# Head stacks through memory, the output projection in halves, the context laid out by features

## The chip, the cores and the metric

The kernel runs on one core of a Trainium2 chip (trn2). The metric is the device time of one execution in microseconds (us), as the median of several runs. The core has five engines with a queue each: PE (TensorE, matrix products), DVE (VectorE), ACT (ScalarE), POOL (GpSimd) and SP (SyncE, which here only starts DMA transfers). Instructions of one engine run in the order of its program and wait on semaphores for the others.

## What is computed

A cross attention with 16 heads followed by a mixture of experts, in float32, for 8 batches of 512 tokens with 512 features. Cut to what matters here (`ctx` is the context, the mask is all ones in the data):

```
q = layernorm(x) @ Wq + bq;  k = ctx @ Wk + bk;  v = ctx @ Wv + bv      # 16 heads of 32
attn = softmax(q k^T * 32**-0.5);  x = x + concat_heads(attn v) @ Wo + bo
route_prob = softmax(layernorm(x) @ Ws + bs)                            # 8 experts, each takes its best 512 of 4096 tokens
x = x + scatter_add(route_val * (gelu(xin @ W1 + b1) @ W2 + b2))
```

## The kernel before

Float32 products are made of three products of rounded parts: every operand is kept as a hi part (float32r) and a lo part (what is left), and hi*hi, hi*lo and lo*hi are summed in PSUM. ACT writes the hi part, DVE the lo part.

**Groups.** The attention part goes through 32 groups, a group being one batch and 4 of its 16 heads (128 features). For group g, `proj` makes the transposed projections qT and kT (128 features x 512 tokens, 12 matmuls each). They are then moved into *stacks* `qst` and `kst` (three of each, taken in turn): for each of the 4 heads the stack holds in partitions 0 to 95 three rows of 32: for q hi, lo, hi, and for k hi, hi, lo, so that one matmul over 97 or 99 partitions gives all three products at once, with the mask and the row maxima in the further rows. A feature of head h sits in partition 32h+d of qT and must come to partition d of the stack, so the move is a DMA.

**Per group.** 16 `max` matmuls give scores by query, DVE takes the extreme of each row (`nmax`), ACT sums the exps (`sum`, L979); the maxima go through a transpose (`rows`) and a small DMA into the q stack. Then come 16 `score` matmuls, transposed, whose exps ACT writes to `p_ring` (L991), four to each of the steps kt = 0 to 3, and `att` adds p times v into `ps_att`, four heads at a time. `divide` and `osplit` leave the group's features in `oT`. One period of the kernel is a batch of four groups.

**Output.** When all four groups of batch b are done, `out` (48 matmuls in four tiles of 128 tokens) multiplies oT by Wo, DVE adds the residual, SP stores the sum, DVE normalises in place (`x1_norm`, which waits until the store has landed), and the routing logits follow (`route`, `logits`, `back`).

**Order.** All engines read one list of steps, the agenda, and each performs its own part of every step. A function places the steps of projections, output, loads and transposes at times given as fractions of a group (`K_AT`, `Q_AT`, `LATE_AT` and so on), between the fixed pattern of `score` and `att`. PSUM has one bank for `att` and seven that all other steps take in turn. In the period of the rows below, the late steps of batch 3 stand in group 16, the loads and transposes for batch 5 in groups 17 and 18, and the q stack of group 20, the first of batch 5, is made in group 18.

**Queues.** SP starts the q stack (L713 and L717), the stores `out_x` (L751) and `hn_rows` (L757), and the passage of the softmax denominators through memory (`rden`). POOL starts the k stack (L887, L891) and the loads of x and of the context, adds the bias to the residual (L843) and does the inverse roots of the norms (L782).

## Time and profile before

| | |
|---|---|
| median of 3 runs | 1889.41 us (1887.9 to 1889.69) |
| profiled execution | 1890.99 us, its span 1889.2 us |
| PE, DVE, ACT, POOL busy | 87%, 58%, 52%, 24% of the span |
| attention part | about 0 to 1090 us, a period of 129.7 us per batch |
| expert part | the rest |

The span is that from the first to the last instruction in the trace. "busy" does not say that an engine binds: what matters is in which stage it stands, and what ends its wait. A matmul's duration holds its latency; how fast they follow one another is seen in their starts.

### The profile page before, as it was taken

To read this page: it belongs to the slowest core of one execution; us is meant where nothing else is said; L and a number is where in the kernel's file an instruction comes from. 1 tells how busy PE (TensorE), PEld (TensorE's weight loads), DVE (VectorE), ACT (ScalarE), POOL (GpSimd) and SP (SyncE) were. 2 spreads that over 40 slices of the span, in tenths; PEclk is the share of its full clock that TensorE was granted. 3 is DMA by queue.
4 is the path that set the end of the run, shared out by engine and by line. 5 is a ranking of instruction groups with operands and counts; after the bars stand their busy time and mean duration, and the time that the engine had idled before them with its cause. 6 is when DMAs were issued, how large, how long until landed. Compare 5 with 4: busy or idle time off the path is not lost.

```text
span 1889.2 us, 22557 instructions
## 1 busy us (share of the span) xinstructions
PE 1648.3 (87%) x7795; PEld 1172.2 (62%) x7795; DVE 1097.1 (58%) x1918; ACT 985.9 (52%) x2111; POOL 455.7 (24%) x729
## 2 busy tenths in 40 slices
PE   5778978979879889798798737999999999999996
PEld 4545645536545556455364326878888888888885
DVE  5565675665665756756656364777645554455543
ACT  3688587687686785876876611222323232222321
POOL 4232332423324323324233102010202020202001
PEclk9788998989989989999899957999999999999998
DMA  4233332433424333324334213243434242515331
GB/s 158 80 98 82 101 112 63 132 90 80 146 53 122 106 82 106 107 63 129 92 81 130 85 51 112 90 118 112 140 110 141 90 139 90 163 67 162 95 106 23
DMA packets 122538, 193.99 MB, mean 103 GB/s; under 512 B 25020, under 2 KB 59472, under 8 KB 122424
## 3 DMA queue, kind: packets, MB, share of 16 engines
q1 hardware_dynamic: 93560, 125.79, 20.6%
q0 software_dynamic: 28864, 66.75, 14.0%
q8 instruction: 63, 1.03, 0.2%
q14 instruction: 51, 0.42, 0.1%
HBM read 116.03 MB, written 25.58 MB: 75 GB/s over the span
## 4 chain that ended last, share of the span: by engine, by line
PE 68%; DVE 9%; ACT 9%; issue 4%; DMA 4%; SPq 3%; POOL 1%; ACTq 0%; DVEq 0%; POOLq 0%
PE ps_gen L652 8%; PE ps_gen L654 8%; PE ps_gen L653 8%; PE ps_gen L1695 6%; PE ps_gen L1697 6%; PE ps_gen L1696 6%; PE ps_gen L1513 5%; ACT ps_gen L979 5%; PE ps_att L1544 5%; PE ps_gen L1533 4%; ACT p_ring L991 3%; PE ps_gen L1499 2%; PE ps_gen L1500 2%; DVE nmax L1151 2%; PE ps_gen L1501 2%
## 5 line engine op out<-in xcount | busy, mean ns | idle before, releaser
L1151 DVE TENSOR_REDUCE nmax<-ps_gen 128x1 f32<-128x512 f32 x512 | 338.7, 682 | 140.7 <-PE ps_gen L1513 139.0
L979 ACT ACTIVATE ps_gen<-ps_gen,nmax 128x512 f32<-128x512 f32 x512 | 342.3, 671 | 134.8 <-DVE nmax L1151 133.1
L991 ACT ACTIVATE p_ring<-ps_gen,keep_scale 128x512 f32<-128x512 f32 x512 | 339.1, 693 | 87.4 <-PE ps_gen L1533 85.7
L1041 ACT ACTIVATE gel<-ps_gen,b_cols 128x512 f32<-128x512 f32 x128 | 88.3, 690 | 450.7 <-PE ps_gen L654 450.6
L1513 PE MATMUL ps_gen<-kst,qst 97*128 97x512 f32 x512 | 231.0, 466 | 75.6 <-issue 51.6
L1398 DVE TENSOR_TENSOR gel_lo<-gel,gel_hi 128x512 fp32r<-128x512 f32 x126 | 87.2, 692 | 288.3 <-ACT gel_hi L1042 288.3
L1513 PEld LDWEIGHTS ps_gen<-kst,qst 97*128 97x128 f32 x512 | 104.4, 205 | 175.9 <-issue 121.1
L1533 PE MATMUL ps_gen<-qst,kst 99*128 99x512 f32 x512 | 192.1, 426 | 18.1 <-DMA qst<-by_row 11.9
L652 PE MATMUL ps_gen<-hT_hi,w_hi 128*128 128x512 f32 x512 | 203.1, 397 | 1.5 <-DVE hT_lo L1391 1.5
L654 PE MATMUL ps_gen<-hT_hi,w_lo 128*128 128x512 f32 x512 | 200.3, 391 | 0.0
L653 PE MATMUL ps_gen<-hT_lo,w_hi 128*128 128x512 f32 x512 | 200.3, 391 | 0.0
L1695 PE MATMUL ps_gen<-w_hi,gel_hi 128*128 128x512 f32 x504 | 198.3, 393 | 0.0
L887 POOL DMA_DIRECT2D kst<-kT_hi x256 | 126.8, 503 | 296.0 <-ACT kT_hi L962 160.6
L1697 PE MATMUL ps_gen<-w_hi,gel_lo 128*128 128x512 f32 x504 | 196.6, 390 | 0.0
L1696 PE MATMUL ps_gen<-w_lo,gel_hi 128*128 128x512 f32 x504 | 196.4, 390 | 0.0
L927 POOL DMA_INDIRECT out_x<-y_out,idx x32 | 55.7, 1740 | 583.3 <-ACT y_out L1061 504.8
L1544 PE MATMUL ps_att<-p_ring,v_sb 128*32 128x512 f32 x1024 | 147.4, 649 | 5.0 <-ACT p_ring L991 4.8
L1533 PEld LDWEIGHTS ps_gen<-qst,kst 99*128 99x128 f32 x512 | 97.0, 198 | 49.0 <-issue 21.6
L979 ACT ACTIVATION_READ_ACCUMULATOR ps_gen<-ps_gen,nmax 128x1 f32 x512 | 109.8, 214 | 0.0
L652 PEld LDWEIGHTS ps_gen<-hT_hi,w_hi 128*128 128x128 f32 x512 | 96.7, 189 | 21.0 <-issue 1.9
L654 PEld LDWEIGHTS ps_gen<-hT_hi,w_lo 128*128 128x128 f32 x512 | 96.6, 189 | 20.8
L653 PEld LDWEIGHTS ps_gen<-hT_lo,w_hi 128*128 128x128 f32 x512 | 96.7, 189 | 19.4
(199 smaller groups left out, 2777.5 us busy)
## 6 DMA issues: line engine op xcount, KB each, us to landing
w_raw<-in_L_ffn_W SPq DMA_DIRECT2D x128, 512.0 KB, 4.3
kst<-kT_hi POOLq DMA_DIRECT2D x256, 64.0 KB, 1.9
qst<-qT_hi SPq DMA_DIRECT2D x256, 64.0 KB, 2.4
x_in<-in_x POOLq DMA_DIRECT2D x60, 256.0 KB, 3.3
kst<-kT_lo POOLq DMA_DIRECT2D x128, 64.0 KB, 2.2
qst<-qT_lo SPq DMA_DIRECT2D x128, 64.0 KB, 2.0
rden_b<-rden_rows SPq DMA_DIRECT2D x32, 256.0 KB
out_x<-x_in SPq DMA_DIRECT2D x32, 256.0 KB, 2.1
```

The costliest lines, as they stand in the source:

```text
L652: e.matmul(psum, lhsT=wh, rhs=mh, start=(i == 0), stop=False)
L653: e.matmul(psum, lhsT=wh, rhs=ml, start=False, stop=False)
L654: last = e.matmul(psum, lhsT=wl, rhs=mh, start=False, stop=(i == n - 1))
L979: e.activation(psum[:, :], psum[:, :], ACT.Exp, bias=nmax[g % 2][:, c], scale=-1.0, accum_out=den[g % 2][:, c]).then_inc(drained_sem("max" ...
L991: e.activation(p_ring[n % NP_][:, :], ps("score", g, kt, h)[:, :], ACT.Exp, scale=keep_scale[:, b:b + 1]).then_inc(drained_sem("score", g, ...
L1151: e.tensor_reduce(nmax[g % 2][:, h * TB + t:h * TB + t + 1], ps("max", g, h, t)[:, :], AX.X, ALU.min).then_inc(s_min, 1)
L1513: e.matmul(ps("max", g, h, t)[:, :], lhsT=qst[k][0:ROWS_MAX, h, t * P:(t + 1) * P], rhs=kst[k][0:ROWS_MAX, h, :], start=True, stop=True).t ...
L1533: e.matmul(ps("score", g, kt, h)[:, :], lhsT=kst[k][0:ROWS_ALL, h, kt * P:(kt + 1) * P], rhs=qst[k][0:ROWS_ALL, h, :], start=True, stop=Tr ...
L1544: last = e.matmul(ps_att[h * DH:(h + 1) * DH, :], lhsT=v_sb[:, kt, (c4 * HG + h) * DH:(c4 * HG + h + 1) * DH], rhs=p_ring[((g * KT + kt) * ...
L1695: e.matmul(ps_y[tt], lhsT=gh, rhs=wh, start=(j == 0), stop=False)
L1696: e.matmul(ps_y[tt], lhsT=gh, rhs=wl, start=False, stop=False)
L1697: return e.matmul(ps_y[tt], lhsT=gl, rhs=wh, start=False, stop=(j == NF - 1))
```

## The change

It has three parts and new numbers in the placing. **Stacks:** each projection is stored in two DMAs of 128 x 512 (hi, lo) to a buffer `qk_rows` in device memory, two of them in turn for q and for k, and comes back in three loads of 32 x 4 x 512 that lay the heads beside each other; it was eight hi and four lo copies of 32 x 512 from SBUF to SBUF. The loads wait until the store has landed. **Halves:** `outa` makes the product of the first two feature blocks of a batch in its groups r = 2 and after, and DVE adds it to the residual; `out` makes the second two, and has 6 matmuls per tile instead of 12. **Context:** it is handed over transposed by the host, so each 128 x 512 tile of features is split by ACT and DVE straight from its landing place (`csplit`), without the transposes on PE.

```diff
+            if step[0] == "proj_lo":
+                self.add("stack", *step[1:])
...
-    K_AT = ((0.07, 0.17), (0.04, 0.22), (0.03, 0.15), (-0.07, 0.33))
-    Q_AT = ((0.33, 0.45), (0.23, 0.27), (0.33, 0.45), (0.12, 0.43))
+    K_AT = ((0.07, 0.38), (-0.04, 0.22), (0.05, 0.15), (-0.07, 0.18))
+    Q_AT = ((0.41, 0.43), (0.23, 0.27), (0.33, 0.37), (0.14, 0.35))
...
-    RECIP_AT, RDEN_AT, RDEN_IN_AT = 0.0, 0.05, 0.6
+    RECIP_AT, RDEN_AT, RDEN_IN_AT = -0.02, 0.28, 0.75
...
-    LATE_AT = (("residual", 0.05), ("add_bias", 0.2), ("out", 0.32), ("x1_norm", 0.44),
-               ("route", 0.57), ("logits", 0.68), ("back", 0.74))
+    HALF_AT, HALF_FOR = (("residual", 0.25), ("add_bias", 0.34), ("outa", 0.49)), 0.79
+    LATE_AT = (("out", 0.13), ("x1_norm", 0.46), ("route", 0.57), ("logits", 0.66), ("back", 0.74))
...
+        if r == 2:
+            for kind, at in HALF_AT:
+                place(i, (at, at + HALF_FOR), [(late, kind, b, t) for t in range(TB)])
...
-    for t in range(TB):
-        a.residual(B - 1, t)
-    for t in range(TB):
-        a.add("add_bias", B - 1, t)
...
+        def keep_rows(e, on, w, g):
+
+            if g >= 2:
+                on.wait_ge(s_stack_hi[w][(g - 2) % NST], 32 * ((g - 2) // NST + 1))
+                on.wait_ge(s_stack_lo[w][(g - 2) % NST], 16 * ((g - 2) // NST + 1))
+            kept = qk_rows["qk".index(w), g % 2]
+            on.wait_ge(s_proj_hi[w], g + 1)
+            e.dma_start(kept[0], raw(qk[w, "hi"][:, :])).then_inc(s_kept_hi[w], 16)
+            on.wait_ge(*drained("proj", w, g))
+            e.dma_start(kept[1], raw(qk[w, "lo"][:, :])).then_inc(s_kept_lo[w], 16)
+
+        def load_stack(e, on, w, g):
+
+            k = g % NST
+            stack, rows_hi, row_lo = (qst, (0, 2), 1) if w == "q" else (kst, (0, 1), 2)
+            kept = [qk_rows["qk".index(w), g % 2, n].rearrange("(h d) s -> d h s", d=DH) for n in range(2)]
+            on.wait_ge(s_ones_rows[k], 2)
+            if g >= NST:
+                on.wait_ge(*full("score", g - NST, KT - 1, HG - 1))
+            on.wait_ge(s_kept_hi[w], 16 * (g + 1))
+            for r in rows_hi:
+                e.dma_start(raw(stack[k][r * DH:(r + 1) * DH, :, :]), kept[0]).then_inc(s_stack_hi[w][k], 16)
+            on.wait_ge(s_kept_lo[w], 16 * (g + 1))
+            e.dma_start(raw(stack[k][row_lo * DH:(row_lo + 1) * DH, :, :]), kept[1]).then_inc(s_stack_lo[w][k], 16)
...
+                elif kind == "csplit":
+                    b, c = at
+                    on.wait_ge(*tile_landed("c", b, c))
+                    if b > 0:
+                        on.wait_ge(*full("proj", "k", b * GB - 1))
+                        on.wait_ge(*full("v", b - 1, TB - 1))
+                    e.activation(cT[0][:, c, :], tile_in("c", b, c), ACT.Copy).then_inc(s_c_hi, 1)
...
-                        on.wait_ge(*full("out", b - 1, TB - 1))
+                        on.wait_ge(*full("outa" if c4 < GB // 2 else "out", b - 1, TB - 1))
...
+                elif kind == "outa":
+                    b, t = at
+                    n, x1 = b * TB + t, x_in[residual_slot(b, t)]
+                    on.wait_ge(*full("outa", b, t))
+                    on.wait_ge(s_x1, n + 1)
+                    e.tensor_tensor(x1[:, :], ps("outa", b, t)[:, :], x1[:, :], ALU.add).then_inc(drained_sem("outa", b, t), 1)
```

How this moves PE between the last q projection of group 20 and the first max of that group. Before (L1501 is the last matmul of the projection, L1513 max, L1533 score, L1544 att, L1520 the transpose of the maxima; the last row is the first max of group 20):

```order
L1501 MATMUL ps_gen<-xT_hi,wq_lo 128x512
L1513 MATMUL ps_gen<-kst,qst 128x512
L1533 MATMUL ps_gen<-qst,kst 128x512 x2
L1513 MATMUL ps_gen<-kst,qst 128x512
L1544 MATMUL ps_att<-p_ring,v_sb 32x512 x4
L1513 MATMUL ps_gen<-kst,qst 128x512
L1533 MATMUL ps_gen<-qst,kst 128x512 x2
L1520 MATMUL ps_gen<-ident,nmax 16x128
L1533 MATMUL ps_gen<-qst,kst 128x512 x2
L1513 MATMUL ps_gen<-kst,qst 128x512
```

Of the change, from the att step of the same stretch on (max is now L1545, score L1565, att L1576, and L1592 to L1594 are outa; ahead of the rows shown stand three max and three score matmuls behind the projection, and one max; each outa tile has the three lines twice):

```order
L1545 MATMUL ps_gen<-kst,qst 128x512
L1576 MATMUL ps_att<-p_ring,v_sb 32x512 x4
L1592 MATMUL ps_gen<-wo_hi,oT_hi 128x512
L1593 MATMUL ps_gen<-wo_lo,oT_hi 128x512
L1594 MATMUL ps_gen<-wo_hi,oT_lo 128x512
...
L1545 MATMUL ps_gen<-kst,qst 128x512
L1565 MATMUL ps_gen<-qst,kst 128x512 x2
L1552 MATMUL ps_gen<-ident,nmax 16x128
L1565 MATMUL ps_gen<-qst,kst 128x512 x2
L1592 MATMUL ps_gen<-wo_hi,oT_hi 128x512
...
L1545 MATMUL ps_gen<-kst,qst 128x512
```

Two tiles of outa now stand between the projection and the max, and one more max and score matmul. On SP's queue around the q stack of group 18, before:

```order
L751 DMA out_x<-x_in0 128x512
L713 DMA qst0<-qT_hi 32x512 x8
L717 DMA qst0<-qT_lo 32x512 x4
L757 DMA hn_rows<-x_in0 128x512
L751 DMA out_x<-x_in1 128x512
L738 DMA rden_b<-rden_rows 128x1x512
L757 DMA hn_rows<-x_in1 128x512
```

Of the change:

```order
L771 DMA out_x<-x_in0 128x512
L749 DMA rden_rows<-by_row 16x128
L739 DMA kst0<-mask_rows 1x4x512
L771 DMA out_x<-x_in1 128x512
L612 DMA qk_rows<-qT_hi 128x512
L614 DMA qk_rows<-qT_lo 128x512
L626 DMA qst0<-qk_rows 32x4x512 x2
L628 DMA qst0<-qk_rows 32x4x512
L777 DMA hn_rows<-x_in0 128x512
L771 DMA out_x<-x_in2 128x512
L777 DMA hn_rows<-x_in1 128x512
L758 DMA rden_b<-rden_rows 128x1x512
```

The stack now stands behind the second store of x1 where it stood behind the first, and in front of both normalised tiles. On POOL's queue the context loads stand around the k stack of group 19 in the change like this:

```order
L848 DMA x_in2<-in_ctx_1024 128x512
L612 DMA qk_rows<-kT_hi 128x512
L614 DMA qk_rows<-kT_lo 128x512
L626 DMA kst1<-qk_rows 32x4x512 x2
L628 DMA kst1<-qk_rows 32x4x512
L848 DMA x_in3<-in_ctx_1024 128x512
L848 DMA x_in0<-in_x 128x512
```

Before, two of the four context loads stood ahead of that stack and two behind it; now three stand ahead and one behind.

## Rows read from the trace of the kernel before

**Rows 1.** The page: span, busy times, and the granted clock in 40 slices.

```profile
span 1889.2 us, 22557 instructions
PE 1648.3 (87%) x7795; PEld 1172.2 (62%) x7795; DVE 1097.1 (58%) x1918; ACT 985.9 (52%) x2111; POOL 455.7 (24%) x729
...
PEclk9788998989989989999899957999999999999998
```

**Rows 2.** Windows, stages A to D: length, busy, PEclk, DMA share, GB/s.

```profile
570.30:605.00 34.70, 32.64 (x156) 22.71 (x156) 19.83 (x36) 23.67 (x54) 12.73 (x23) 1.00 0.36 98
605.00:641.80 36.80, 32.15 (x170) 19.79 (x171) 24.15 (x52) 23.90 (x58) 13.65 (x24) 0.91 0.47 149
641.80:670.20 28.40, 23.07 (x115) 12.91 (x113) 23.38 (x46) 25.44 (x58) 10.95 (x21) 1.00 0.31 75
670.20:700.00 29.80, 23.64 (x103) 14.35 (x104) 14.67 (x24) 23.04 (x55) 6.86 (x14) 0.83 0.26 69
```

**Rows 3.** Timeline of PE in C and D: start, us, idle before in brackets.

```profile
666.03 0.39 PE L1501 MATMUL ps_gen<-xT_hi,wq_lo 128*128 128x512 f32 x1
...
667.43 1.07 PE L1544 MATMUL ps_att<-p_ring,v_sb 128*32 128x512 f32 x8
...
676.69 0.77 PE L1513 MATMUL ps_gen<-kst,qst 97*128 97x512 f32 x1 [5.72 <-issue]
...
687.04 0.40 PE L1499 MATMUL ps_gen<-cT_hi,wk_hi 128*128 128x512 f32 x1
687.27 0.40 PE L1500 MATMUL ps_gen<-cT_lo,wk_hi 128*128 128x512 f32 x1
```

**Rows 4.** Timeline of SP at the q stack of group 20.

```profile
667.54 4.99 SPq L713 DMA_DIRECT2D qst<-qT_hi  x8
672.58 2.49 SPq L717 DMA_DIRECT2D qst<-qT_lo  x4
```

**Rows 5.** Windows behind the two waits, and the one with the wait in B.

```profile
677.00:682.00 5.00, 5.00 (x16) 2.37 (x16) 2.28 (x4) 2.26 (x6) 0.00 (x0) 0.50 0.12 48
...
603.40:615.00 11.60, 7.59 (x43) 4.33 (x42) 6.03 (x14) 4.00 (x11) 4.83 (x7) 0.95 0.52 173
615.00:620.80 5.80, 5.80 (x17) 4.09 (x21) 3.18 (x6) 3.11 (x8) 0.30 (x1) 0.50 0.12 45
```

**Rows 6.** Timeline of SP at the q stack of group 18.

```profile
603.28 2.49 SPq L717 DMA_DIRECT2D qst<-qT_lo  x4
...
607.62 0.43 SPq L751 DMA_DIRECT2D out_x<-x_in  x1
```

**Rows 7.** Timeline of DVE there, and its waits from 259.4 to 1037 us.

```profile
610.71 0.55 DVE L1081 TENSOR_SCALAR x_in<-x_in,mv,rstd 128x512 f32<-128x512 f32 x1 [5.30 <-DMA out_x<-x_in]
...
DVE x_in L1081 <- DMA out_x<-x_in: 32.7, 7, 5.3
```

**Rows 8.** Timeline of PE around that wait.

```profile
604.96 0.27 PE L1520 MATMUL ps_gen<-ident,nmax 128*16 128x128 f32 x1 [1.47 <-DVE nmax L1151]
...
614.89 0.79 PE L1513 MATMUL ps_gen<-kst,qst 97*128 97x512 f32 x1 [1.66 <-ACT ps_gen L979]
```

**Rows 9.** The page's DMA issues: count, KB each, median us from issue to landing.

```profile
x_in<-in_x POOLq DMA_DIRECT2D x60, 256.0 KB, 3.3
...
out_x<-x_in SPq DMA_DIRECT2D x32, 256.0 KB, 2.1
```

**Rows 10.** Groups by line and shape from 259.4 to 1037 us.

```profile
L1465 PE MATMUL ps_gen<-ident,x_in 128*128 128x128 f32 x176 | 27.8, 280 | 16.4 <-ACT ps_gen L979 7.5 <-DVE x_in L1081 5.0 <-DVE cT_lo L1098 3.9
...
L1218 DVE TENSOR_TENSOR x_in<-ps_gen,x_in 128x512 f32<-128x512 f32 x24 | 16.6, 690 | 36.6 <-PE ps_gen L1572 32.7 <-POOL x_in L843 3.7
```

**Rows 11.** Timeline of PE at the end of the attention part.

```profile
1073.84 0.51 PE L1556 MATMUL ps_gen<-wo_hi,oT_hi 128*128 128x512 f32 x1
...
1082.18 0.39 PE L1570 MATMUL ps_gen<-wo_hi,oT_hi 128*128 128x512 f32 x1
```

More of the change, by code:

```diff
@@ L127, in load, with csplit @@
             self.add("load", kind, b, t)
+    def csplit(self, b, c):
+        self.add("csplit", b, c)
+        self.later.append(("csplit_lo", b, c))
     def stats(self, b, t):
@@ L194, in attention_agenda @@
     a = Agenda()
-    for kind in "xc":
-        for t in range(TB):
-            a.load(kind, 0, t)
+    for t in range(TB):
+        a.load("x", 0, t)
+        a.load("c", 0, t)
     for t in range(TB):
         a.stats(0, t)
-        a.turn("c", 0, t)
+        a.csplit(0, t)
         a.flush()
-        a.turn("x", 0, t)
+        a.turn(0, t)
     a.flush()
@@ L262, in late @@
             a.out(b, t)
-        elif kind in ("route", "logits", "back"):
+        elif kind in ("outa", "route", "logits", "back"):
             a.with_bank(kind, b, t)
@@ L333, in attention_agenda @@
         a.flush()
-    for t in range(TB):
-        a.residual(B - 1, t)
-    for t in range(TB):
-        a.add("add_bias", B - 1, t)
     attend(NG - 1, KT - 1)
@@ L722, in sync_program @@
                         e.dma_start(raw(kst[k][ROW_MASK:ROW_MASK + 1, :, :]), src).then_inc(s_mask_row[k], 16)
+                elif kind == "stack" and at[0] == "q":
+                    load_stack(e, on, "q", at[1])
                 elif kind == "rden":
@@ L786, in slot_free @@
                 if was == "first":
-                    on.wait_ge(*full("turn", "x", 0, at[2]))
+                    on.wait_ge(*full("turn", 0, at[2]))
+                elif was == "load" and at[0] == "c":
+                    on.wait_ge(s_c_hi, at[1] * DC + at[2] + 1)
+                    on.wait_ge(s_c_lo, at[1] * DC + at[2] + 1)
                 elif was == "load":
-                    on.wait_ge(*full("turn", *at))
+                    on.wait_ge(*full("turn", *at[1:]))
                 elif was == "wo":
@@ L1546, in tensor_program @@
                     last.then_inc(s_av, 1)
-                elif kind == "osum":
+                elif kind in ("outa", "osum", "out"):
                     b, t = at
+                    first = {"outa": 0, "osum": GB // 2, "out": GB // 2 if b < B - 1 else GB - 1}[kind]
+                    stop = {"outa": GB // 2, "osum": GB - 1, "out": GB}[kind]
+                    key = ("outa" if kind == "outa" else "out", b, t)
                     cols = slice(t * P, (t + 1) * P)
-                    on.wait_ge(*free("out", b, t))
-                    on.wait_ge(s_ol, GB * (b + 1) - 1)
+                    if kind != "out" or b < B - 1:
+                        on.wait_ge(*free(*key))
+                    on.wait_ge(s_ol, GB * b + stop)
@@ L1575, in tensor_program @@
+                        e.matmul(ps(*key)[:, :], lhsT=oh, rhs=w_hi["o"][:, c, :], start=(c in (0, GB // 2)), stop=False)
+                        e.matmul(ps(*key)[:, :], lhsT=oh, rhs=w_lo["o"][:, c, :], start=False, stop=False)
+                        last = e.matmul(ps(*key)[:, :], lhsT=ol, rhs=w_hi["o"][:, c, :], start=False, stop=(c in (GB // 2 - 1, GB - 1)))
+                    if kind != "osum":
+                        last.then_inc(full_sem(*key), 1)
                 elif kind == "route":
@@ L1762 @@
             a = np.ascontiguousarray(a.reshape(-1, 128).T)
+        if name == 'ctx_1024':
+            a = np.ascontiguousarray(a.transpose(0, 2, 1))
         arrays[f"in_{name}"] = a
```

156 lines of the change are left out of this document (60 added, 96 removed).

## The prediction

> **What bounds the kernel now.** The page first: one execution of 1889.2 us, PE busy for 87%, and a granted TensorE clock that sags all through the first 1070 us, the attention part [rows 1]. The expert part behind it is not touched. The attention part repeats every 129.7 us, one batch of four groups of heads. I cut one period at the transposes of the row maxima and read it in windows [rows 2]: stage A (34.7 us: projections, v, two output tiles), B (36.8: two output tiles, routing, context), C (28.4: x, projections), D (29.8: projections, v of the next batch). No stage is ruled by one engine throughout. A is PE: 32.6 of 34.7. C is ACT: 25.4 of 28.4, 90%. B and D are not full on anything: B has PE 32.2, ACT 23.9 and DVE 24.2 of 36.8, D has PE 23.6 and ACT 23.0 of 29.8. So B and D hold time that a wait takes, and I looked for the waits.
>
> In D: PE ends the last q projection of the next batch at 666.4, does 3 to 4 us of other work and stands for 5.7 us before the first max matmul of that group, until 676.69 [rows 3]. The max needs all twelve stack transfers. SP issues eight for 4.99 us from 667.54 and four for 2.49 us from 672.58 [rows 4]; the first wait is 1.1 us behind PE, the stack then takes 9.15. The stall costs twice: from 677 to 682 PE is full at a granted clock of 0.50 (1.2 GHz of 2.4) [rows 5], while later, at 1.00, matmuls start 0.23 us apart [rows 3]. Five microseconds at half speed are 2.5 lost. Together 8.2 us, seven times (once per batch with a successor).
>
> In B: the same SP queue is still issuing stack transfers when an x1 tile is ready, so its store starts at 607.62 behind L717 and a store [rows 6]. DVE may normalise only when that store has landed: it stands 5.30 us, until 610.71, in front of everything queued on it, nmax reductions included [rows 7]. PE stands 1.47 us before and 1.66 behind that wait [rows 8], and 4.0 us in all from 603.4 to 615, then works 5.8 us at clock 0.50 [rows 5], 2.9 lost. DVE's wait adds up to 32.7 us in the six periods that I grouped [rows 7].
>
> **The change, part by part.**
>
> *Stacks.* q goes by SP, k by POOL: two stores of 256 KB to memory and three loads of 256 KB in place of twelve copies of 64 KB. Issue time on SP falls from 7.5 us [rows 4] to about five times 0.62, 3.1 us. The path is now two landings in series. From the nearest rows, a 256 KB store lands in 2.1 us and a load in 3.3 [rows 9]: hi store 2.1, two hi issues 1.25, then the lo load 3.3, makes 6.65 us in place of 9.15 (the lo store, begun 0.9 later, lands at 3.0 and hides). The other bound: the store of rows 6 and 7 took 3.1 us, which gives 7.65; if both landings grow by 2 us, 10.65. I take 6.65, by the medians. The k stacks have nobody waiting at present and I cost them at nothing; the cover is most of a stage. The memory traffic added, 64 times 512 KB in 1040 us, is 32 GB/s on 69 to 149 [rows 2]: nothing, except in the full part of B. The first sum stands by these rows alone.
>
> The Trainium skill speaks against this edit: "DMA: Bandwidth & Descriptors", Anatomy of one DMA, puts about 2 us fixed on each DMA and says that waiting for the write receipt can be surprisingly long when the target is HBM, which the old on-chip copies did not have. By its fit (2.0 us and bytes over 436 GB/s) a landing is 2.6 us and the path, as an estimate, 2.6 + 1.25 + 2.6 = 6.45. The rows agree in size (2.1 and 3.3); what the old path lost was issue time.
>
> *Cover of the wait in D.* Between the last q projection and the first max PE had nine 128x512 matmuls and one att step, 9 x 0.23 + 1.0 + 0.1 = 3.2 us. Now two outa tiles stand there too, and the q projections are two matmuls earlier: 24 x 0.23 + 1.1 = 6.6 us. Stack at 1.1 + 6.65 = 7.75: PE idles 1.1 instead of 5.7. I take the clock to hold there: stage A keeps 1.00 with 2.1 us of idle in it [rows 2]. D: -4.6 - 2.5, and plus 18 matmuls of outa (4.2) that now lie in D: -2.9. PE work alone of 27.8 (98 matmuls, four att steps, 1.0 small) at A's share of 0.94 would be 29.6, a floor above that; so D is 28.5 to 29.6, take 28.8: -1.0. C gets one outa tile (six matmuls, 1.4 us) while ACT rules: +0.5.
>
> *Halves.* 48 output matmuls per batch stay 48, 24 of them out of A and B into C and D. A loses 7 of 106 matmuls net: -1.6, and PE's 1.5 us wait at its end: A -2.5 (part is kept as gaps). B loses 18 of 80. DVE gains 4 adds of 0.69 us per batch [rows 10], 2.8 us in C and D, where DVE is busy 23.4 of 28.4 and 14.7 of 29.8; it is hidden in D, and costs up to 1 us in C, within the +0.5. In B the q stack is issued behind x1's second store, and SP is free of it in 4 us; the norms come a step later. DVE's 5.3 us wait goes, and with it PE's and the clock: 4.0 + 2.9 - 1.5 (already in A) = 5.4; half of the 18 matmuls, 2.1; a new stack wait as in D, since the halved tiles cover less there too (22 matmuls): +1.1. Sum -6.4, B = 30.4. ACT at C's 90% would put it at 26.6, so no floor is hit.
>
> *Context by features.* 16 transposes per batch leave PE (280 ns each with their latency [rows 10], about 0.12 apart), 1.9 us in B, of which half was path: -0.9. The ACT and DVE passes remain, same count and tile size. But ACT now waits for a load instead of PE, in its own queue with the exps. The fourth context load stands on POOL behind the k stack; by the old issue times POOL is clear of that about when it was, so I cost it at 0, and as a rival below.
>
> *Numbers moved.* rden_in at 0.75 leaves the load one step, some 7 us, for 3.3. Cost nothing.
>
> *Tail.* After the last att step PE has 36 osum matmuls, 1073.84 to 1082.18, 8.3 us [rows 11]; now 12, 2.8 us, and the last division and split need about the same 2.8: -5.5. The outa tiles lie under exps there. *Head.* The first max of all has only the first q stack ahead of it, on the same path: 9.15 to 6.65, -2.5.
>
> Sum per period: A -2.5, B -7.3, C +0.5, D -1.0 = -10.3; seven times -72; tail and head -8. Total -80. The profiled execution took 1890.99 around its span, the median is 1889.41; the sum goes from the median: 1809. Two of its terms (B's and the head's) assume that nothing second stands behind the wait removed. In each stage the second wait is usually there, so I give back a quarter of B's gain, 7 x 1.8 = 13: **1822 us**.
>
> **The rivals.**
>
> *A second wait in B and D.* Removing SP's delay uncovers DVE, which in B already has 24.2 us of work in a fixed order with PE and ACT. Then half of B's and all of D's gain is lost: per period -5.6, seven times -39, and -8: 1842. For: rows 2 show no engine above 90% in B without the waits. Against: the two waits named are on the chain.
>
> *The landings are slow.* If each takes 2 us longer, the stack takes 10.65 and PE idles 5.1 us before the first max, with 2.5 more behind it for the clock: +6.5 at a place. At both places that is +13 against -10.3, 1900. In B the DMA queues are fuller (149 GB/s against 69 in D [rows 2]), so the likelier form is B alone: -3.8 per period, 1854. For: the 3.1 us store of B. Against: the medians.
>
> *Context on ACT's queue (slower).* If the context loads land late, ACT stands with its exps queued behind, and PE and DVE wait for those. It waits for the k stack on POOL, for a slot that is free only when the hn store has landed, and then 3.3 us. A lateness of 3 us for each of four tiles costs 12 us and 2.5 for the clock, 14.5 against 10.3: +29 in seven periods, less 8, is 1910. It decides from 11.5 us per period (80 over 7). For: POOL is a strict queue and its next item is a wait on a landing. Against: three of the four loads stand ahead of the k stack, up to half a group before their split; only the last is close.
>
> *Nothing changes*: ACT, 96.1 us of 129.7 by the sum of rows 2, is far from binding, so only an exact cancelling gives it.
>
> **How the numbers follow.** Forecast, B and D as worked out, 0.52 (its own range 1795 to 1832); second wait 0.25; slow landings in B 0.11; slower 0.08; nothing 0.04. The range starts at 1790: 1809 less 13 if D reaches its 26.9 us, and some 6 for its floor in C. It ends at 1868, past the slow landings at 1854 by half of a second place (the 46 us between 1854 and 1900, a third of it). What is left out is the slower case and the tails. A difference under 0.2% can't be told from none by this measurement. Faster 0.88, same 0.04, slower 0.08.
>
> **What would show it.** A period near 120 us. In D, PE's wait before the first max near 1 us and clock 1.00 behind it; in B no DVE wait on the x1 store; SP's stack issues near 3 us per group; landings of qk_rows stores near 2.1. osum near 2.8 us. Wrong if the wait before the first max is over 4 us, or ACT stands before csplit.

## The result and the profile after

The changed kernel takes 1834.49 us, median of four runs from 1831.13 to 1851.74, against 1888.66 (four runs from 1884.94 to 1889.69) on the same chip: a ratio of 0.9735, 95% interval 0.9673 to 0.9798. That is 54 us less, where 1822 had been forecast and 1790 to 1868 was the range. The same kernel timed once more beside the last experiments gave 1836.66 (six runs), ratio 0.9744 [0.9717, 0.9771]. The profiled execution took 1831.13 us.

The page of the changed kernel, the lines that answer to [rows 1], and the one on all DMA traffic:

```profile
span 1829.2 us, 21959 instructions
PE 1621.5 (89%) x7667; PEld 1158.9 (63%) x7667; DVE 1111.6 (61%) x1950; ACT 987.3 (54%) x2111; POOL 357.9 (20%) x505
...
PEclk9789989999899899898998859999999999999998
...
DMA packets 127653, 227.46 MB, mean 124 GB/s; under 512 B 17852, under 2 KB 52304, under 8 KB 127544
```

PE lost 128 matmuls, the 16 context transposes of each of eight batches, and is a little fuller; the clock digits still sag in the attention part.

The stages, cut at the same transposes as [rows 2], then one window behind the wait in D and one in B (length, busy time of PE, PEld, DVE, ACT and POOL, granted clock, DMA share, GB/s); the last two rows are the six periods of the table below, before and after:

```profile
547.70:577.50 29.80, 28.33 (x138) 19.32 (x137) 21.41 (x40) 22.11 (x50) 5.50 (x10) 1.00 0.26 87
577.50:608.70 31.20, 25.44 (x144) 14.38 (x144) 23.61 (x51) 24.59 (x59) 8.21 (x15) 0.93 0.68 214
608.70:639.50 30.80, 26.86 (x114) 15.77 (x114) 22.69 (x44) 26.00 (x60) 9.10 (x15) 0.80 0.42 119
639.50:670.70 31.20, 29.39 (x132) 19.95 (x133) 16.47 (x27) 23.71 (x55) 8.60 (x12) 0.95 0.44 132
645.00:651.00 6.00, 6.00 (x20) 4.58 (x19) 3.55 (x7) 4.84 (x12) 2.10 (x3) 0.72 0.33 87
599.80:606.00 6.20, 4.59 (x19) 1.91 (x17) 5.19 (x14) 4.92 (x12) 2.19 (x5) 0.84 1.00 292
...
181.00:959.80 778.80, 669.05 (x3242) 418.80 (x3242) 492.54 (x942) 576.46 (x1327) 262.68 (x480) 0.93 0.35 99
...
176.30:916.60 740.30, 652.79 (x3146) 411.51 (x3145) 502.85 (x966) 577.55 (x1326) 189.02 (x312) 0.93 0.46 138
```

This period is 123.0 us long in place of 129.7. Two stages fell, A by 4.9 and B by 5.6; two grew, C by 2.4 and D by 1.4. D is now a full stage: PE busy 29.4 of 31.2, with 132 instructions where it had 103. B's DMA share went from 0.47 to 0.68.

**The clock gave nothing back.** D's granted clock rose from 0.83 to 0.95, but C's fell from 1.00 to 0.80, behind PE's stands late in B. Length times what the clock lacks, from these rows and [rows 2], is 3.3 (B) and 5.1 (D) before, 8.4 us a period, and 2.2, 6.2 and 1.6 (B, C, D) after, 10.0 us. Over the six periods the granted clock is 0.93 in both kernels.

One period is one sample, so here are the means of six (from the fifth group of heads to the twenty-ninth, cut at the start of each group's row-maxima transposes in PE's timeline; us). The columns from the third on belong to experiments below. Each column is read from one profiled execution; for "q by memory" and "k by memory" (only that stack goes through memory) it was the slowest of four, 1823.4 and 1823.7 us.

| stage | before | after | stacks copied | q by memory | k by memory | extra stores | no halves | context through PE | old numbers |
|---|---|---|---|---|---|---|---|---|---|
| A | 34.7 | 29.8 | 29.9 | 29.8 | 29.9 | 30.2 | 31.8 | 29.9 | 36.0 |
| B | 36.8 | 32.5 | 30.4 | 31.6 | 32.0 | 33.4 | 35.9 | 36.9 | 29.3 |
| C | 28.6 | 30.2 | 30.6 | 31.5 | 29.1 | 30.3 | 28.6 | 29.1 | 31.1 |
| D | 29.7 | 30.9 | 31.0 | 29.5 | 31.6 | 30.4 | 29.4 | 30.1 | 32.5 |
| sum | 129.8 | 123.4 | 121.9 | 122.4 | 122.6 | 124.3 | 125.7 | 126.0 | 128.9 |

**The wait in D**, PE's timeline at the first max matmul of group 20, where [rows 3] showed 5.72 us:

```profile
641.18 0.39 PE L1594 MATMUL ps_gen<-wo_hi,oT_lo 128*128 128x512 f32 x1
643.38 0.47 PE L1545 MATMUL ps_gen<-kst,qst 97*128 97x512 f32 x1 [1.81 <-issue]
...
645.60 0.63 PE L1545 MATMUL ps_gen<-kst,qst 97*128 97x512 f32 x1
...
648.52 0.40 PE L1593 MATMUL ps_gen<-wo_lo,oT_hi 128*128 128x512 f32 x1
648.75 0.39 PE L1594 MATMUL ps_gen<-wo_hi,oT_lo 128*128 128x512 f32 x1
```

SP's timeline of the same stack, which answers to [rows 4]:

```profile
634.03 0.34 SPq L612 DMA_DIRECT2D qk_rows<-qT_hi  x1
634.87 0.34 SPq L614 DMA_DIRECT2D qk_rows<-qT_lo  x1
636.54 0.81 SPq L626 DMA_DIRECT2D qst<-qk_rows  x2
637.39 0.43 SPq L628 DMA_DIRECT2D qst<-qk_rows  x1
```

SP now issues for 1.9 us in all, where it issued for 7.5. But from the first issue at 634.03 to the max at 643.38 pass 9.35 us; before it was 9.15 from 667.54. At the first max of the six batches in the table it is 8.8 to 9.8 us, before 9.1 to 9.4. In this kernel the path did not become shorter. The idle time did, from 5.72 to 1.81, with output matmuls (L1592 to L1594) now standing in front of the max. The last load of the stack lands 5.8 us after its issue. Beside it runs a load of x for the residual, which the halves moved into this stage:

```profile
637.17 0.58 POOL L859 DMA_DIRECT2D x_in<-in_x  x1
```

Where that load is absent, in two kernels below, the same path takes 7.2 to 8.0 us. Behind that max the matmuls still start 0.42 us apart at 645.60 and 0.23 apart at 648.52: the clock was at half for some 3.5 us even after 1.81 us of idleness.

The page's DMA issues (count, KB each, median us from issue to landing), against [rows 9]:

```profile
kst<-qk_rows POOLq DMA_DIRECT2D x96, 256.0 KB, 4.1
qst<-qk_rows SPq DMA_DIRECT2D x96, 256.0 KB, 4.0
x_in<-in_x POOLq DMA_DIRECT2D x60, 256.0 KB, 4.6
...
qk_rows<-qT_hi SPq DMA_DIRECT2D x32, 256.0 KB, 3.0
qk_rows<-qT_lo SPq DMA_DIRECT2D x32, 256.0 KB, 4.1
```

The forecast had 2.1 for the stores and 3.3 for the loads. The stores of k, issued by POOL, stayed nearer to it (2.3 for hi and 2.5 for lo). The x loads, whose size and engine are the same as before, rose from 3.3 to 4.6.

**The waits** of the six periods (176.3 to 916.6 us; us in total, times, longest):

```profile
PE ps_gen L1552 <- DVE nmax L1176: 32.2, 18, 6.5
PE ps_gen L1545 <- issue: 30.5, 16, 5.1
...
ACT cT_hi L966 <- DMA x_in<-in_ctx: 14.7, 6, 5.5
...
DVE x_in L1243 <- POOL x_in L866: 20.9, 8, 3.6
```

DVE's wait for the x1 store [rows 7] is gone from the list. In its place stands a new chain in B. The chain of work, from stage B on (start, us, what):

```profile
595.27 2.28 DMA qk_rows<-kT_hi
...
598.14 0.94 POOL kst L626 x2
...
599.80 6.21 DMA x_in<-in_ctx
606.03 0.64 ACT cT_hi L966
606.69 0.69 DVE cT_lo L1124
607.38 1.21 DVE nmax L1176 x2
609.10 0.85 PE ps_gen L1565 x2
```

POOL stores k, waits for the landing, issues three loads for the k stack and only then the fourth context load; that one takes 6.21 us, with q's stores and loads (from 599.18 on SP) and three x loads beside it, with a DMA share of 1.00 from 599.80 to 606.00. ACT and DVE do their context split in front of the max reductions, and PE waits for those.

The tail, PE's timeline, against [rows 11]:

```profile
1020.86 0.50 PE L1592 MATMUL ps_gen<-wo_hi,oT_hi 128*128 128x512 f32 x1
...
1024.89 0.39 PE L1594 MATMUL ps_gen<-wo_hi,oT_lo 128*128 128x512 f32 x1
1028.84 1.08 PE L1604 MATMUL ps_gen<-ident,x_in 128*128 128x128 f32 x4 [3.56 <-DVE x_in L1101]
```

Twelve osum matmuls and the first six of the last column take from 1020.86 to 1024.89.

### The profile page after: what moved, and what is told of

Same layout as the page of the kernel before. It is cut to its first block, busy times and chain, and to the rows that moved or that the text cites. A ratio compares the mean times of both kernels' runs of the same rounds, so it can differ in the third digit from the quotient of the medians.

```text
span 1829.2 us, 21959 instructions
## 1 busy us (share of the span) xinstructions
PE 1621.5 (89%) x7667; PEld 1158.9 (63%) x7667; DVE 1111.6 (61%) x1950; ACT 987.3 (54%) x2111; POOL 357.9 (20%) x505
## 2 busy tenths in 40 slices
DMA packets 127653, 227.46 MB, mean 124 GB/s; under 512 B 17852, under 2 KB 52304, under 8 KB 127544
## 4 chain that ended last, share of the span: by engine, by line
PE 73%; DMA 9%; DVE 6%; ACT 5%; issue 4%; POOL 1%; SPq 0%; POOLq 0%; ACTq 0%; DVEq 0%
PE ps_gen L677 8%; PE ps_gen L679 8%; PE ps_gen L678 8%; PE ps_gen L1718 6%; PE ps_gen L1720 6%; PE ps_gen L1719 6%; PE ps_att L1576 6%; PE ps_gen L1545 6%; PE ps_gen L1565 4%; PE ps_gen L1531 3%; DMA qst<-qk_rows 3%; PE ps_gen L1532 2%; PE ps_gen L1533 2%; DMA x_in<-in_ctx 2%; ACT ps_gen L999 2%
## 5 line engine op out<-in xcount | busy, mean ns | idle before, releaser
L1545 PE MATMUL ps_gen<-kst,qst 97*128 97x512 f32 x512 | 232.0, 470 | 58.3 <-issue 37.2
L1545 PEld LDWEIGHTS ps_gen<-kst,qst 97*128 97x128 f32 x512 | 106.6, 209 | 179.3 <-issue 122.8
L1565 PE MATMUL ps_gen<-qst,kst 99*128 99x512 f32 x512 | 200.5, 442 | 17.7 <-ACT ps_gen L999 12.9
L1576 PE MATMUL ps_att<-p_ring,v_sb 128*32 128x512 f32 x1024 | 150.5, 662 | 3.6 <-ACT p_ring L1011 3.6
L1565 PEld LDWEIGHTS ps_gen<-qst,kst 99*128 99x128 f32 x512 | 102.1, 207 | 49.5 <-ACT ps_gen L999 21.4
L1720 PEld LDWEIGHTS ps_gen<-w_hi,gel_lo 128*128 128x128 f32 x504 | 94.6, 188 | 20.0
```

The lines of the kernel that those rows point to most:

```text
L1545: e.matmul(ps("max", g, h, t)[:, :], lhsT=qst[k][0:ROWS_MAX, h, t * P:(t + 1) * P], rhs=kst[k][0:ROWS_MAX, h, :], start=True, stop=True).t ...
L1565: e.matmul(ps("score", g, kt, h)[:, :], lhsT=kst[k][0:ROWS_ALL, h, kt * P:(kt + 1) * P], rhs=qst[k][0:ROWS_ALL, h, :], start=True, stop=Tr ...
L1576: last = e.matmul(ps_att[h * DH:(h + 1) * DH, :], lhsT=v_sb[:, kt, (c4 * HG + h) * DH:(c4 * HG + h + 1) * DH], rhs=p_ring[((g * KT + kt) * ...
L1720: return e.matmul(ps_y[tt], lhsT=gl, rhs=wh, start=False, stop=(j == NF - 1))
```

## The experiments

Numbers are medians in us with the range of the runs; the ratio is to the kernel before on the same chip. Where two variants are compared, the difference is given both by medians and by ratios, since the chips differ a little. The one with extra stores does additional work.

### The stacks alone: put into the kernel before, taken out of the kernel after

Into the kernel before, only the path through memory (keep_rows and load_stack, and the stack step behind proj_lo):

```diff
+            if step[0] == "proj_lo":
+                self.add("stack", *step[1:])
...
-                        for h in range(HG):
-                            for r in (0, 2):
-                                e.dma_start(raw(qst[k][r * DH:(r + 1) * DH, h, :]), raw(qk["q", "hi"][h * DH:(h + 1) * DH, :])
+                        keep_rows(e, on, "q", g)
```

> The kernel before with the stacks through memory and nothing else. Theory 1: DVE's wait of 5.3 us for the x1 store and PE's of 5.7 us before the first max both shrink, 1860 to 1875 us. Rival: 1885 or more, since the second landing in series takes the place of the issue time.

Measured: 1891.14 (1882.03 to 1893.96, ten runs), ratio 1.0008 [0.9987, 1.0029]. No change. Its waits, 259 to 1000 us:

```profile
PE ps_gen L1526 <- issue: 28.4, 8, 4.3
PE ps_gen L1526 <- DMA qst<-qk_rows: 23.8, 8, 4.0
...
DVE x_in L1094 <- DMA out_x<-x_in: 12.6, 7, 2.6
```

Its first issue of the q stack of group 20 on SP, and PE's first max of that group:

```profile
667.35 0.34 SPq L615 DMA_DIRECT2D qk_rows<-qT_hi  x1
...
674.65 0.76 PE L1526 MATMUL ps_gen<-kst,qst 97*128 97x512 f32 x1 [3.92 <-issue]
```

**Here the path is shorter**: 7.3 us instead of 9.15 (7.2 to 7.7 at the first max of six batches), and PE stands 3.9 us before that max where it stood 5.7. The rival was right on the time and not on the reason: the second landing did not take the place of the issue time at this spot.

SP is free sooner, and it shows: DVE's wait for the x1 store is 12.6 us where it was 32.7 [rows 7], and stage B is 31.8 us on the mean of six periods against 36.8. But A is 38.2 against 34.7 and C 31.4 against 28.6 (D 28.2 against 29.7): the sum, 129.6, is that of before. PE waits 52.2 us in front of max matmuls, 23.8 of it named as loads of the stack. The gain of B and D was real and was taken back in A and C: before the first max of the second and of the fourth group of a batch PE stands 2.7 and 3.1 us on the mean, where it stood 0.6 and 0.2.

Out of the kernel after, everything else kept, the twelve on-chip copies in load_stack:

```diff
-            for r in rows_hi:
-                e.dma_start(raw(stack[k][r * DH:(r + 1) * DH, :, :]), kept[0]).then_inc(s_stack_hi[w][k], 16)
+            for h in range(HG):
+                for r in rows_hi:
+                    e.dma_start(raw(stack[k][r * DH:(r + 1) * DH, h, :]), raw(qk[w, "hi"][h * DH:(h + 1) * DH, :])
+                                ).then_inc(s_stack_hi[w][k], 16)
```

> The changed kernel with the stacks made by twelve copies from SBUF to SBUF again (issued at the step where the loads from memory stand now); halves, context and numbers stay. Theory 1 (SP's and POOL's issue time is the cost that the stacks' part removes, and it is worth about a third of the 54 us although its landings are slow): 1845 to 1860 us, SP issues 7.5 us per stack again, and the wait before the first max of a batch grows above the 1.8 us that it has in the changed kernel. Rival (the passage through memory costs more than it gives, since its stores land in 3 to 4 us and its loads in 4, with the DMA engines full): 1825 or less, and the cold stretch behind the context loads is gone.

Measured: 1819.5 (1818.14 to 1820.01, four runs), ratio 0.9628 [0.9605, 0.9652]. This beats both kernels, as the rival had it. Its sign did not come: the granted clock in C is 0.84 on the mean of six periods, and 0.83 in the changed kernel. The memory path costs 15 us by medians, 20 by ratios (17 and 22 against the second timing of the changed kernel). Its SP and PE at group 20:

```profile
621.14 5.01 SPq L617 DMA_DIRECT2D qst<-qT_hi  x8
626.19 2.49 SPq L621 DMA_DIRECT2D qst<-qT_lo  x4
...
630.27 0.47 PE L1539 MATMUL ps_gen<-kst,qst 97*128 97x512 f32 x1 [1.57 <-issue]
```

Twelve copies arrive in 9.13 us, PE idles 1.57. So in D the two ways are equal, 9.13 and 9.35. The difference lies in B (table: 30.4 and 32.5). The window of its six periods, against that of the changed kernel above (176.30 to 916.60):

```profile
170.80:901.90 731.10, 652.01 (x3147) 409.97 (x3145) 502.87 (x966) 578.37 (x1326) 265.52 (x480) 0.93 0.38 105
```

Same work, granted clock 0.93 in both, 9.2 us apart, and PE's busy time is the same too. Another 5.5 us lie ahead of these windows, in the first batch (176.3 against 170.8), and some 2.8 come back behind them: the spans, 1829.2 and 1817.3, are 11.9 apart. Its waits:

```profile
PE ps_gen L1539 <- issue: 31.0, 17, 4.2
PE ps_gen L1546 <- DVE nmax L1170: 23.1, 18, 2.2
...
ACT cT_hi L960 <- DMA x_in<-in_ctx: 2.5, 4, 1.7
...
DVE x_in L1237 <- POOL x_in L860: 10.7, 8, 2.7
```

PE's wait for the stacks is equal (30.5 and 31.0); its wait for nmax is 9.1 us longer in the changed kernel, and so are the waits that feed it: ACT's for the context load by 12.2, DVE's for POOL's residual by 10.2.

### Which of the two queues

The same edit for one of the two alone (COPIED = "k" or "q" in front of the branches):

```diff
+COPIED = "k"
...
+            if w == COPIED:
+                return
```

> The changed kernel with the k stacks copied from SBUF to SBUF and the q stacks through memory. Theory 1 (the passage through memory costs 15 us because the k stacks and their traffic delay the context loads, which stand on the same queue): close to the version with both copied, 1817 to 1824 us. Theory 2 (it costs because the q stack has two landings in series in front of PE): 1828 to 1836.

> The mirror: q stacks copied, k stacks through memory. Theory 1: as slow as the changed kernel, 1830 to 1836 us, with the context loads landing late and the clock down behind them. Theory 2: 1817 to 1824.

Measured: q through memory, k copied, 1819.75 (1817.08 to 1823.41), ratio 0.9641 [0.961, 0.9672]; k through memory, q copied, 1819.72 (1816.35 to 1823.67), ratio 0.9639 [0.9605, 0.9673]; four runs each. Either alone costs nothing beside copying both; only the two together do. So neither theory holds: the first failed on the mirror, the second on the first of the two. The page puts the traffic at 193.96 MB with both copied, 210.71 MB with one through memory, 227.46 with both. In the table each alone already lengthens B (31.6 and 32.0 for 30.4) and wins it back next door: q through memory in D (29.5), k through memory in C (29.1). PE's waits with q alone through memory, 172.9 to 906.9 us:

```profile
PE ps_gen L1568 <- DVE nmax L1192: 38.4, 18, 5.7
...
PE ps_gen L1561 <- issue: 6.1, 7, 1.4
```

The wait for the stack nearly disappears there, 6.1 for 31.0, and the wait for nmax takes 15 us of the 25. ACT's wait for the context load is 14.2 us in this kernel and 12.3 in the other, nearly what it is in the changed kernel (14.7), and both are as fast as the copied version. So that wait alone doesn't make the 15 us.

### Is it the late context load?

The split, and with it the x loads and statistics that share its slots and queue, somewhat later:

```diff
-    LOAD_C_AT, SPLIT_C_AT = (-0.18, 0.33), (0.35, 0.49)
-    LOAD_X_AT, NORM_X_AT, TURN_X_AT = (0.50, 0.74), (0.62, 1.03), (0.99, 1.16)
+    LOAD_C_AT, SPLIT_C_AT = (-0.18, 0.33), (0.43, 0.57)
+    LOAD_X_AT, NORM_X_AT, TURN_X_AT = (0.58, 0.80), (0.70, 1.05), (0.99, 1.16)
```

> The changed kernel with the context's split 0.08 of a group (some 2.5 us) later, and the loads and norms of x 0.08 later behind it. Theory 1 (ACT waits for a late context load and that holds the exps): 1822 to 1830 us, ACT's waits for context loads (13.4 us in six batches) gone. Rival (that wait lies beside other work): 1831 to 1840.

Measured: 1831.94 (1827.63 to 1839.26, four runs), ratio 0.9723 [0.9682, 0.9764]. Not to be told from the changed kernel. ACT's waits, 180 to 960 us:

```profile
ACT cT_hi L966 <- DMA x_in<-in_ctx: 3.2, 2, 2.6
```

The wait went from 14.7 to 3.2 us and the time stayed (B 32.4, C 30.4, D 30.2). The late context load is on the chain of the period shown, but it is not what the 15 us hang on; what stands behind it was not found. (The edit also moved the x loads, and the four runs spread over 12 us, so a gain of a few us would not be seen.)

### Is it the bytes?

The copied version, with the two stores of 256 KB per projection kept behind the copies, to where nobody reads them (additional work, and the projections' tiles are held until the stores have landed):

```diff
+            kept = qk_rows["qk".index(w), g % 2]
+            e.dma_start(kept[0], raw(qk[w, "hi"][:, :])).then_inc(s_kept_hi[w], 16)
+            e.dma_start(kept[1], raw(qk[w, "lo"][:, :])).then_inc(s_kept_lo[w], 16)
```

> The version with copied stacks, to which two stores of 256 KB to memory per projection are added that nobody reads; the buffers qT and kT are free only when they have landed. It moves as many bytes as the changed kernel (1280 KB per stack) but has no second landing ahead of PE. If traffic is the cost: 1828 to 1836 us. If the order of two landings is the cost: 1818 to 1823.

Measured: 1848.46 (1845.14 to 1851.32, four runs), ratio 0.9795 [0.9761, 0.9829]: 29 us more than without them by medians, 32 by ratios, and above what either theory had said. Half of it is lost in the first batch already (the fifth group's transposes of row maxima begin at 185.8 us, against 170.8), 14.3 in the six periods. Its traffic is that of the changed kernel, 227.54 MB, no max matmul needs a second landing, and PE's wait in front of the max is small (9.0 us, for nmax 49.0). ACT's wait for the context loads is 18.6 us. So a second landing on the path is not needed to lose time. But it is no clean measure of bytes: the stores also take issue time on SP and POOL and may delay the loads behind them. Bytes or places in the queue stay unseparated.

### The halves

The changed kernel with the output projection whole, at the output's old numbers:

```diff
-    HALF_AT, HALF_FOR = (("residual", 0.25), ("add_bias", 0.34), ("outa", 0.49)), 0.79
-    LATE_AT = (("out", 0.13), ("x1_norm", 0.46), ("route", 0.57), ("logits", 0.66), ("back", 0.74))
-    LATE_FOR = 0.74
+    LATE_AT = (("residual", 0.05), ("add_bias", 0.2), ("out", 0.32), ("x1_norm", 0.44),
+               ("route", 0.57), ("logits", 0.68), ("back", 0.74))
+    LATE_FOR = 0.72
...
-                    first = {"outa": 0, "osum": GB // 2, "out": GB // 2 if b < B - 1 else GB - 1}[kind]
+                    first = {"osum": 0, "out": 0 if b < B - 1 else GB - 1}[kind]
```

> The changed kernel with the output projection whole again, its late steps at the numbers of before; stacks through memory, context by features and the other numbers stay. Theory 1 (halves carry the larger part: they fill PE's wait in D and relieve A and B): 1855 to 1870 us, the wait before the first max of a batch back at 4 us or more. Rival (halves only move work to where PE is as full): within 5 us of the changed kernel.

And the same with the stacks copied:

> The version with copied stacks without the halves (output whole, its late steps at the old numbers). Theory A: the halves are worth 20 us or more here too, 1840 to 1860 us, with PE's wait before the first max of a batch back near 4 us or more, since nothing covers the stack's 9 us. Rival (the halves gained only because they covered the slow passage through memory): within 8 us of 1820.

Measured: stacks through memory 1853.73 (1851.92 to 1858.66, four runs), ratio 0.9819 [0.9792, 0.9846]; stacks copied 1853.35 (1852.48 to 1857.78, four runs), ratio 0.9832 [0.9805, 0.9858]. Halves are thus worth 19 us by medians (16 by ratios) with stacks through memory and 34 (39) with stacks copied. Without halves the way of the stacks makes no difference, as in the kernel before. B is 35.9 us without halves; a reading that no run tests is that a stage so full of output work doesn't feel its transfers.

PE's first max of group 20 without halves, stacks through memory:

```profile
649.56 0.77 PE L1546 MATMUL ps_gen<-kst,qst 97*128 97x512 f32 x1 [2.60 <-issue]
```

The two expectations named 4 us or more for this wait. It is 2.9 us on the mean of six batches with stacks through memory, where the path takes 7.4 to 8.0 us, and 4.3 with stacks copied, where it takes 9.1 to 9.5. With halves the two are 1.8 and 1.3 us. So halves cover more of the wait with stacks copied (3.0 us) than through memory (1.1 us), where the path grows by some 1.7 us when they come in. The residual's x loads beside it fit that, but they were not moved by themselves.

### The context

The context taken by tokens and transposed on PE again, at the places of the split:

```diff
     def csplit(self, b, c):
-        self.add("csplit", b, c)
-        self.later.append(("csplit_lo", b, c))
+        key = ("cturn", b, c)
+        self.take_bank(key)
+        self.add(*key)
+        self.put_late(key, ("csplit_lo", b, c))
```

> The changed kernel with the context by tokens and transposed on PE again, at the same places as the split has now. Theory 1 (16 transposes of 0.12 us per batch, partly on the path): 1838 to 1845 us. Rival (the split from the landing place makes ACT wait for late loads, so the part costs): 1830 or less, with no wait of ACT for a context load.

Measured: 1850.23 (1846.99 to 1858.44, four runs), ratio 0.9801 [0.9765, 0.9837]: 16 us above the changed kernel by medians, 12 by ratios (14 and 11 against the second timing, whose interval just touches this one; that of the first overlaps it). It is above both expectations, and ACT's wait for context loads is gone, but only because PE has it. PE's waits, 180 to 960 us:

```profile
PE ps_gen L1507 <- DMA x_in<-in_ctx: 31.0, 6, 8.9
```

With the transposes back it is PE that stands for the late load, up to 8.9 us and with all its queue behind it; B is 36.9. PE's idle time in B is 8.6 us a period, against 5.2, while 16 transposes at 0.12 us are 1.9. So the layout seems to pay less by the matmuls it saves than by letting ACT, which has slack, take the wait. A kernel with transposes would have put them later, so this is the price at these places.

### The numbers

The copied version with the numbers of before for everything but the output (K_AT to NORM_X_AT):

```diff
-    K_AT = ((0.07, 0.38), (-0.04, 0.22), (0.05, 0.15), (-0.07, 0.18))
-    Q_AT = ((0.41, 0.43), (0.23, 0.27), (0.33, 0.37), (0.14, 0.35))
+    K_AT = ((0.07, 0.17), (0.04, 0.22), (0.03, 0.15), (-0.07, 0.33))
+    Q_AT = ((0.33, 0.45), (0.23, 0.27), (0.33, 0.45), (0.12, 0.43))
...
-    V_AT, V_NEXT_AT = (-0.02, 0.78), (0.36, 1.32)
-    LOAD_C_AT, SPLIT_C_AT = (-0.18, 0.33), (0.35, 0.49)
+    V_AT, V_NEXT_AT = (0.21, 0.33), (0.36, 1.36)
+    LOAD_C_AT, SPLIT_C_AT = (-0.01, 0.42), (0.42, 0.95)
```

> The version with copied stacks, halves and context by features, with the placing numbers of the kernel before (projections, v, loads, norms, maxima, denominators; the context's split stands where its transposes stood; the output's late steps keep the new numbers). Theory A (halves and context carry the 70 us between the kernel before and the copied version, the numbers only fit them in): 1822 to 1835 us. Rival (the numbers are a large part): 1845 or more.

Measured: 1876.2 (1874.22 to 1880.85, seven runs), ratio 0.9942 [0.9921, 0.9963], as the rival had it. That is 57 us above the same kernel with the new numbers (59 by ratios) and only about 10 below the kernel before. A is 36.0 in place of 29.9, and PE stands 4.3 us before the first max of a batch in place of 1.3. Its wait there, 259 to 1000 us:

```profile
PE ps_gen L1539 <- issue: 39.4, 20, 4.9
```

The converse, the new numbers with neither halves nor the new context, was not run. The nearest is the version above with stacks copied and no halves: new numbers (all but the output's) and the new context, 1853.35, some 33 us below the kernel before.

One number of the new ones by itself, the q projections of the second group of a batch apart from the k stack:

```diff
-    Q_AT = ((0.41, 0.43), (0.23, 0.27), (0.33, 0.37), (0.14, 0.35))
+    Q_AT = ((0.41, 0.43), (0.40, 0.44), (0.33, 0.37), (0.14, 0.35))
```

> The changed kernel with the q projection of r = 1 moved from 0.23 of the group to 0.40, so that its stack's 1280 KB do not pass beside the k stack's and the context loads. If the 12 to 15 us that the passage through memory costs come from DMA crowding in that one place: 1822 to 1829 us. If they are spread over many places, or the x loads are crowded instead: within 4 us of the changed kernel.

Measured: 1842.88 (1837.94 to 1845.63, five runs), ratio 0.9765 [0.9742, 0.9788]. B fell to 31.4 us and C rose to 33.2. Parting the two stacks relieves B, and the later q makes the next group late; the time is 6 us above the changed kernel beside it, with overlapping intervals. It fits neither branch of the expectation: parting those two stacks in this way doesn't win back the 15 us.

The changed kernel, unedited, on the chip of the last four:

> The changed kernel once more, unedited, beside these, to have its time with more runs: 1832 to 1837 us by both theories; 1826 or less would make the 15 us between it and the copied version a matter of scatter.

Measured: 1836.66 (1827.95 to 1843.14, six runs), ratio 0.9744 [0.9717, 0.9771]. The median stands where both theories had it, so the 15 us are not scatter.

## Why the prediction was right, and where its steps were not

Direction was right, and the size nearly: 54 us less where 67 had been forecast. 1834.5 lies in the stated range, but just outside the 1795 to 1832 that the forecast's own case had, and its stages look more like the first rival (half of B's gain and all of D's lost, 1842). The largest single gains are in A and B, which lost output matmuls; the reason named for D, more PE work in front of the max, is seen in the wait there and not in D's length. Several terms were wrong and cancelled, so a part of the hit is luck.

**Where 60 us of span went.** To the first row-maxima transposes 1.8 (56.4 us to 54.6); from there to the last group's 49.4 (996.9 to 947.5); from there to the last att step 1.8; the osum stretch 5.4 (the transposes behind it moved by 58.4 us, from 1087.26 to 1028.84, the last att step by 53.0, from 1072.85 to 1019.87); behind it 1.6. The forecast had 72 for the periods before its allowance of 13, 5.5 for the tail and 2.5 for the head. The tail was right. The head's 1.8 is there with copied stacks too (54.6), so it isn't the shorter path it was credited to.

**Clock: failed, the largest miss among the terms of the sum.** "Together 8.2 us" and "2.9 lost" put 2.5 us in D and 2.9 in B on the clock, 5.4 a period, some 38 of the 72 us (D's floor gave a part of that back). None came in the profiled execution: what the clock lacks costs 8.4 us in the period shown before and 10.0 after, and 0.93 is granted in both over six periods (0.94 when the changed kernel was timed again). The half-speed stretch moved from D into C. PE's idle time per period fell from 18.3 to 14.6 us, and 16 transposes at 0.12 are gone: that is 5.6 of the 6.4 us. The sum took the removal of a wait for the removal of the slow stretch behind it, though PE still stands for 1.2, 2.2 and 1.7 us up to 603.1, 608.7 and 611.7, late in B and early in C.

**Stacks: failed in this kernel.** "Hi store 2.1, two hi issues 1.25, then the lo load 3.3, makes 6.65 us in place of 9.15". It is 9.35. The estimate was fair for the edit by itself: in the kernel before it gives 7.3, near the first bound of 7.65, with the hi store at 2.0 and the lo load at 4.3. What it left out is the other parts of the same change: with the halves in, the path is 9.35. The medians were those of a kernel without these transfers. The issue part was right, even high: SP issues for 1.9 us, not 3.1. The landings of q grew to 3.0 and 4.0 or more (medians), and the last load is issued at 637.39 and used 6.0 us later. "I cost them at nothing" of the k stacks holds alone (k through memory costs nothing beside copies), and not together with q. The value lies between the two upper bounds in the text, 7.65 and 10.65. In this kernel the edit costs 15 to 22 us rather than giving what the shorter path was credited with, and in the kernel before it gives nothing (1891.14 against 1889.62).

The Trainium skill's warning, cited above from "DMA: Bandwidth & Descriptors", Anatomy of one DMA, that a write receipt can be surprisingly long when the target is HBM, bears on this. Its fit, which that page states for DMAs issued from GpSimd, gave 2.6 us for a transfer as an estimate. The stores that POOL issues agree (2.3 and 2.5), those of SP do not (3.0 and 4.1), nor do the loads (4.0). Since x loads, whose target is on the chip, grew as well (3.3 to 4.6), receipt alone isn't what the trace shows.

**Cover: right in kind.** Idle went from 5.72 to 1.81 us (1.1 forecast) on a path that did not shorten, so between these two kernels the cover gave all of it. Taken apart, it is less clean: without halves the wait is 2.9 us already, by a shorter path and earlier q projections. With and without halves the difference in time is 16 to 19 us. "I take the clock to hold there" failed: at half for about 3.5 us.

**Stage D, −1.0: failed in sign** (+1.4, and +1.2 on the mean). PE's work there was put at 27.8 us; it is 29.4. Of the instructions of a period B lost 26 and A 18, D got 29; the forecast had moved 18. The wait was removed and the room filled.

**A −2.5, B −7.3, C +0.5** came as −4.9, −5.6, +2.4 in the period shown, and as −4.9, −4.3, +1.6 on the mean. Period: −10.3 forecast, −6.4 on the mean. B lost its old wait for the x1 store as said, and got the new chain over POOL's k stack and the fourth context load. This is the mechanism of the third rival: its chain is real, at 14.7 us in six periods on ACT's queue, not the 12 us per period it needed to make the kernel slower. The "quarter of B's gain given back", 1.8 a period, was a choice without a row; the mean shows 3.0 of 7.3.

**Context, 0.9 a period: too small.** 11 to 16 us at these places, 1.6 to 2.3 a period over seven; the likely reason is which engine waits for the late load.

**The signs.** Period 123 for 120; issues 1.9 us per stack for 3; no wait of DVE for the x1 store, and osum 2.8 us, as said; stores at 3.0 and 4.1 (q) for 2.1; clock not 1.00 behind the max. One of the two signs of being wrong did come: ACT stands before csplit.

**"Numbers moved. Cost nothing": failed.** The copied version loses 57 to 59 of its 67 to 70 us without them. The halves and the context at the old numbers give some 10. That doesn't make 57 us the worth of the numbers alone: with the new numbers, taking out the halves costs 34 to 39 us (stacks copied) and taking out the context 12 to 16 (stacks through memory), so the parts need one another. A's extra 2.4 us of gain is here in part (A also lost 18 instructions, not 7, and is 31.8 without halves): A is 29.8 with every variant at the new numbers and halves, and 36.0 at the old ones.

**Open.** Why either stack queue through memory is free and both cost 15 us or more: B's crowding at a DMA share of 1.00 is seen, the two loads that cross there are seen, and neither the bytes nor the queue places were isolated. A late context load by itself is ruled out by the runs with one stack through memory. Which of the moved numbers carry the 57 us was not separated, and what they would give the kernel before was not run.

## What to carry to other kernels

Price a rerouted transfer with the landing times of the kernel that will have it: extra copies of the data slow their own landings and their neighbours', and the fullest stretch pays. When a change comes with new placing numbers, treat those as an edit of their own; here halves and context gave some 10 us at the old numbers, and together with the new numbers 70; how much of that the numbers would give alone is not known. A stall can be shortened by ready work in front of it or by a shorter path, and the two are told apart by timing the path and the idle time separately. Don't count a slow-clock stretch as won with the wait in front of it: add up the granted clock over the whole period, before and after.

## What the runs showed of the hardware that was not expected

- Landings of one size in one kernel spread widely with load: 256 KB x loads 3.3 us (median) before, 3.6 with stacks copied, 4.6 with them through memory; one context load took 6.21 us while the DMA share was 1.00, at 292 GB/s.
- Five transfers of 256 KB in two serial landings and twelve on-chip ones of 64 KB took the same in kernels with the halves, 9.35 and 9.13 us, and 7.3 and 9.15 us in the kernel before; for SP the first are 1.9 us of issuing and the others 7.5.
- The granted clock fell to 0.50 behind an idle time of only 1.81 us, when PE had stood only for 0.26 and 0.77 us in the 8 us before that, and was at 0.50 for some 3.5 us.
- Removing the wait in front of a half-speed stretch did not remove the stretch from the period: D's clock went from 0.83 to 0.95 and C's from 1.00 to 0.80, the six periods stayed at 0.93.
- Stores that nobody reads, 64 times 512 KB, cost 29 us, their issue time and the longer hold on their buffers included.
